# Other PSUM banks for the key norms, the query norms and the value transposes of two attention layers

## The reference

```python
x = x + attn_a(layernorm(x))   # q,k,v = z @ w(1024->64) @ fc(64->1024) + b ; 16 heads of 64
x = x + ffn(layernorm(x))      # 1024 -> 4096, gelu, -> 1024
x = x + attn_b(layernorm(x))   # q,k,v = x @ w_qkv ; 16 heads of 64
x = x + ffn(layernorm(x))

scores = einsum('bihd,bjhd->bhij', q, k) / 8
attn   = softmax(scores, axis=-1)
out    = einsum('bhij,bjhd->bihd', attn, v) @ fco_w + fco_b
```

## Time and profile before

| | us |
|---|---|
| profiled execution, its own time | 3357.94 |
| its span, first to last instruction, slowest core (6) | 3356.5 |
| spans of the eight cores | 3337.6 to 3356.5 |
| timed runs | 3369.16 and 3596.16, median 3482.66 |

### The profile page before, as it was taken

The page is one execution under the profiler, slowest core; times in us unless marked ns, Lnnn a source line. Parts: engine busy times, 40 slices in busy tenths (PEclk is TensorE's granted clock), DMA queues, the critical chain, the costliest instruction groups (busy, mean ns, idle before and its releaser), DMA issues.

```text
span 3356.5 us, 33712 instructions; the slowest of 8 cores (3337.6 to 3356.5 us)
## 1 busy us (share of the span) xinstructions
PE 2611.3 (78%) x10548; PEld 911.5 (27%) x10664; DVE 1121.0 (33%) x1570; ACT 1601.9 (48%) x1800; POOL 64.3 (2%) x122
## 2 busy tenths in 40 slices
PE   5557878687865698898947878787787863989999
PEld 1111222122221243343313322222222221334344
DVE  4543445344433021210253334444444432112010
ACT  2248989798920313212213239894898800320310
POOL 0000000000000000000000000000000000000000
PEclk8657999799987899999968889999899996999999
DMA  3000000000004625224001110001000017533532
GB/s 114 0 1 8 5 3 5 2 5 4 4 14 76 120 37 101 51 51 76 1 13 26 20 26 4 4 4 28 4 4 4 5 20 134 102 70 72 104 72 51
DMA packets 36263, 121.01 MB, mean 36 GB/s; under 512 B 7936, under 2 KB 12032, under 8 KB 26880
## 3 DMA queue, kind: packets, MB, share of 16 engines
q0 software_dynamic: 20832, 97.53, 16.9%
q1 hardware_dynamic: 12384, 12.93, 1.3%
q10 hardware_dynamic: 2880, 8.39, 0.7%
HBM read 203.50 MB, written 8.39 MB: 63 GB/s over the span
## 4 chain that ended last, share of the span: by engine, by line
PE 57%; ACT 16%; DVE 11%; DMA 7%; issue 6%; another core or an unknown queue 3%; DVEq 0%; ACTq 0%; SPq 0%; POOLq 0%; POOL 0%
ACT POOL L469 13%; PE PS_A L694 5%; PE PS_A L408 5%; PE PS_A L721 5%; PE PS_B L721 5%; PE PS_B L694 5%; DMA POOL<-w_h 5%; PE PS_C L484 3%; PE PS_D L721 3%; PE PS_D L484 3%; DVE sstat L139 2%; PE PS_C L488 2%; DVE SCR L139 2%; PE PS_E L488 2%
## 5 line engine op out<-in xcount | busy, mean ns | idle before, releaser
L469 ACT ACTIVATE POOL<-PS_A,ebias 128x1024 bf16<-128x1024 f32 x512 | 570.4, 1114 | 104.3 <-PE PS_C L488 40.8
L469 ACT ACTIVATE POOL<-PS_B,ebias 128x1024 bf16<-128x1024 f32 x512 | 570.2, 1114 | 21.6 <-PE PS_C L488 8.1
L694 PE MATMUL PS_A<-BIG,POOL 128*128 128x512 bf16 x1000 | 250.8, 393 | 155.3 <-DMA POOL<-w_h 128.1
L143 ACT ACTIVATE BIG<-PS_A,bcols 128x512 bf16<-128x512 f32 x144 | 98.9, 687 | 557.2 <-PE PS_A L694 543.5
L408 PE MATMUL PS_A<-BIG,POOL 64*128 64x512 bf16 x512 | 196.3, 383 | 102.3 <-ACT POOL L469 100.7
L694 PE MATMUL PS_B<-BIG,POOL 128*128 128x512 bf16 x1004 | 243.9, 383 | 1.2 <-issue 0.2
L408 PE MATMUL PS_B<-BIG,POOL 64*128 64x512 bf16 x512 | 196.1, 383 | 58.8 <-ACT POOL L469 56.9
L139 DVE SCALAR_TENSOR_TENSOR X<-PS_A,bcols,X 128x512 f32<-128x512 f32 x56 | 42.0, 750 | 587.2 <-PE PS_A L721 461.1
L484 PE MATMUL PS_C<-POOL 128*65 128x512 bf16 x512 | 213.2, 416 | 30.4 <-DVE SCR L139 30.4
L139 DVE RECIPROCAL PF<-SCR 33x512 f32<-33x512 f32 x64 | 214.1, 3345 | 67.3 <-DMA SCR<-PF 67.3
L484 PE MATMUL PS_D<-POOL 128*65 128x512 bf16 x512 | 206.9, 404 | 6.1 <-ACT POOL L469 6.1
(11 more groups left out here) (154 smaller groups left out, 3009.6 us busy)
## 6 DMA issues: line engine op xcount, KB each, us to landing
POOL<-w_h POOLq DMA_DIRECT2D x64, 1024.0 KB, 8.8
POOL<-w_h POOLq DMA_DIRECT2D x2, 8192.0 KB, 54.7
X<-xT SPq DMA_DIRECT2D x4, 1024.0 KB, 22.0
X<-xT ACTq DMA_DIRECT2D x4, 1024.0 KB, 25.2
BIG<-POOL SPq DMA_DIRECT2D x64, 64.0 KB, 1.9
POOL<-wqkv_kv POOLq DMA_DIRECT2D x16, 256.0 KB, 4.2
POOL<-wqkv_q POOLq DMA_DIRECT2D x16, 256.0 KB, 3.5
yT<-X SPq DMA_DIRECT2D x16, 256.0 KB, 2.4
```

Of the source, the lines that this page charges most:

```text
L143: return p.inc(getattr(nc.scalar, name)(*a, **k), "act", 1)
L469: nc.scalar.activation(psb, PSx[:, :], AF.Exp, bias=ebias[:, c:c + 1], scale=0.125),
L694: tt = nc.tensor.matmul(PSx[:, ucoff:ucoff + 512], wg[:, dc * 512 + j * 128: dc * 512 + j * 128 + 128], BIG2[:, hoff(dc):hoff(dc) + 512], ...
```

## The change

In `emit_knorm` all four slices go into one bank, PS_E, and each matmul waits for the maximum of the slice before it. The wait for everything issued to TensorE stays only in the first chunk; later chunks wait for named matmuls of the chunk before. `emit_vtranspose` goes through three banks, PS_C low, PS_C high and PS_D, and waits in each round for whoever last read that bank, over the passes too; its wait at the start for everything on VectorE stays only in the first chunk. The query norms alternate between the two banks of PS_A in place of PS_D and PS_E.

```diff
+        vt_bank_ev = {}
+        def emit_vtranspose(vts_off, cpair, entry=False):
-            p.wait(nc.tensor, "dve")
             p.wait(nc.tensor, "act")
+            if entry:
+                p.wait(nc.tensor, "dve")
+            banks = [PS_C[:, 0:512], PS_C[:, 512:1024], PS_D[:, 0:512]]
             for r4 in range(4):
-                boff = (r4 % 2) * 512
-                if r4 >= 2:
-                    p.wait(nc.tensor, round_eng[r4 - 2], round_ev[r4 - 2])
+                bi = r4 % 3
+                g = vt_bank_ev.get(bi)
+                if g is not None:
+                    p.wait(nc.tensor, g[0], g[1])
...
+                vt_bank_ev[bi] = ("dve" if r4 % 2 == 0 else "act", v)

+        kn_prev = {}
         def emit_knorm(cpair, sq_off):
-            p.wait(nc.scalar, "te")
+            if cpair == 0:
+                p.wait(nc.scalar, "te")
+                kn_prev.clear()
             p.wait(nc.scalar, "dve")
-            psl = [PS_D[0:1, 0:512], PS_E[0:1, 0:512]]
...
-                if sl >= 2:
-                    p.wait(nc.scalar, "te", tmm[sl - 2])
+                g = tmm.get(sl - 2) or kn_prev.get("t%d" % (sl + 2))
+                if g is not None:
+                    p.wait(nc.scalar, "te", g)
                 sq = sop("activation", ksq, kc_ap, AF.Square)
                 p.wait(nc.tensor, "act", sq)
-                if sl >= 2:
-                    p.wait(nc.tensor, "dve", mx[sl - 2])
-                tmm[sl] = p.inc(nc.tensor.matmul(psl[sl % 2], ones_b[:, 0:1],
-                                                 ksq, start=True, stop=True),
+                gm = mx.get(sl - 1) or kn_prev.get("m3")
+                if gm is not None:
+                    p.wait(nc.tensor, "dve", gm)
+                tmm[sl] = p.inc(nc.tensor.matmul(PS_E[0:1, 0:512],
+                                                 ones_b[:, 0:1], ksq,
+                                                 start=True, stop=True),
                                 "te", 1)
...
         def emit_qnorm2_and_ebias(sq_off):
-            psl = [PS_D[0:1, 0:512], PS_E[0:1, 0:512]]
+            psl = [PS_A[0:1, 0:512], PS_A[0:1, 512:1024]]
```

More of the change, by code:

```diff
@@ L295, in emit_layernorm_exp @@
             return out
-        def emit_vtranspose(vts_off, cpair):
-            p.wait(nc.tensor, "dve")
+        vt_bank_ev = {}
+        def emit_vtranspose(vts_off, cpair, entry=False):
             p.wait(nc.tensor, "act")
-            round_ev = {}
-            round_eng = {}
+            if entry:
+                p.wait(nc.tensor, "dve")
+            banks = [PS_C[:, 0:512], PS_C[:, 512:1024], PS_D[:, 0:512]]
             for r4 in range(4):
-                boff = (r4 % 2) * 512
-                if r4 >= 2:
-                    p.wait(nc.tensor, round_eng[r4 - 2], round_ev[r4 - 2])
+                bi = r4 % 3
+                g = vt_bank_ev.get(bi)
+                if g is not None:
+                    p.wait(nc.tensor, g[0], g[1])
                 for j in range(4):
                     kt = r4 * 4 + j
-                    psv = PS_C[:, boff + j * 64: boff + (j + 1) * 64].bitcast(BF16)
+                    psv = banks[bi][:, j * 64:(j + 1) * 64].bitcast(BF16)
                     src = POOL[:, vts_off + kt * 128: vts_off + kt * 128 + 128]
@@ L325, in emit_vtranspose @@
                         v = sop("activation", da, sa, AF.Identity)
-                round_ev[r4] = v
-                round_eng[r4] = "dve" if r4 % 2 == 0 else "act"
+                vt_bank_ev[bi] = ("dve" if r4 % 2 == 0 else "act", v)
             return p.cnt["dve"]
+        kn_prev = {}
         def emit_knorm(cpair, sq_off):
-            p.wait(nc.scalar, "te")
+            if cpair == 0:
+                p.wait(nc.scalar, "te")
+                kn_prev.clear()
             p.wait(nc.scalar, "dve")
-            psl = [PS_D[0:1, 0:512], PS_E[0:1, 0:512]]
             tmm = {}
@@ L336, in emit_knorm @@
             for sl in range(4):
-                ksq = POOL[:, (sq_off if sl % 2 == 0 else MB + 8192):
-                           (sq_off if sl % 2 == 0 else MB + 8192) + 512]
+                off = sq_off if sl % 2 == 0 else MB + 8192
+                ksq = POOL[:, off:off + 512]
                 kc_ap = KAR[:, cpair * T + sl * 512: cpair * T + sl * 512 + 512]
-                if sl >= 2:
-                    p.wait(nc.scalar, "te", tmm[sl - 2])
+                g = tmm.get(sl - 2) or kn_prev.get("t%d" % (sl + 2))
+                if g is not None:
+                    p.wait(nc.scalar, "te", g)
                 sq = sop("activation", ksq, kc_ap, AF.Square)
                 p.wait(nc.tensor, "act", sq)
-                if sl >= 2:
-                    p.wait(nc.tensor, "dve", mx[sl - 2])
-                tmm[sl] = p.inc(nc.tensor.matmul(psl[sl % 2], ones_b[:, 0:1],
-                                                 ksq, start=True, stop=True),
+                gm = mx.get(sl - 1) or kn_prev.get("m3")
[4 more added lines that the diff above has]
+                                                 start=True, stop=True),
                                 "te", 1)
                 p.wait(nc.vector, "te", tmm[sl])
-                mx[sl] = vop("reduce_max", S_KSL(sl), psl[sl % 2], axis=AX.X)
+                mx[sl] = vop("reduce_max", S_KSL(sl), PS_E[0:1, 0:512],
+                             axis=AX.X)
             vop("reduce_max", S_KMAX(cpair), sstat[0:1, 16:20], axis=AX.X)
+            kn_prev["t2"] = tmm[2]
+            kn_prev["t3"] = tmm[3]
+            kn_prev["m3"] = mx[3]
         def emit_qnorm2_and_ebias(sq_off):
@@ L812, in build @@
                 p.wait(nc.tensor, "act")
-                emit_vtranspose(OA_VTS, c)
+                emit_vtranspose(OA_VTS, c, entry=(c == 0))
             kv_done = p.cnt["dve"]
@@ L921, in build @@
                 emit_knorm(c, OB_SQ)
-                emit_vtranspose(OB_VTS, c)
+                emit_vtranspose(OB_VTS, c, entry=(c == 0))
             kvb_done = p.cnt["dve"]
```

## The result

| | before | changed kernel |
|---|---|---|
| timed runs, median | 3372.47 us (39 runs) | 3393.64 us (40 runs) |
| profiled execution, its own time | 3357.94 us | 3384.37 us |
| key/value stage, layer A, slowest core | 125.1 us | 139.1 us |
| key/value stage, layer B, slowest core | 195.7 us | 206.4 us |

The ratio of changed to before is 1.0065, with a 95% interval of 1.0049 to 1.0080: slower by 0.65%. The interval leaves out 1, so the change is slower, but by far less than 2%.

The account below looks back on a forecast made before the run. The two key/value stages were taken as chains of handovers with no engine full. 3357.94 + 19.9 - 6.4 + 6.6 = 3378.0 us, +0.6%; range 3354 to 3404 us, 95% within 2% of no change.

Parts of the forecast that it names:

- rival 1: Key norms, both layers: the one-bank turn is hidden and only the gains stay, time 3339.5 us; chance 4%.
- rival 2: Layer B: TensorE's clock stays down, 12.5 us a pass, 100 in eight, time 3478 us; chance 3%.
- rival 3: Whole program: the change is absorbed because something later was waiting anyway, time 3358 us; chance 3%.
- I hold to the profiled execution: Base of the sum: the profiled execution's 3357.94 us, not 3482.66, the median of two unlike timed runs.
- I take 0, in the middle: Layer B, TensorE's clock: cost put at 0 us, between +12 from above and -11 from below.
- Key norms, layer A: One-bank norms: three turns of 1.62 us, last norm matmul 2.49 us later, nothing covers it; eight passes, +19.9 us.
- Third bank, layer A: Transposes: round 2's copies and the next keys come 0.80 us earlier a pass; eight passes, -6.4 us.
- The narrower waits ... are 0 as well: Key norm's start: narrower waits on ScalarE gain nothing, since the remaining VectorE wait covers key copies; 0 us.
- Both edits, layer B: Norms' 2.17 us two thirds paid back by removed wait and third bank; next keys 0.82 later a pass, +6.6 us.
- Query norms: Query norms keep two alternating banks, only others, and the PS_A halves are free then; 0 us.
- The upper bound: Layer B clock: seven more passes with the longer low stretch, 3.4 us dense work at half speed, 1.7 each, +12.
- the predicted signs: Trace marks of being right (turns 1.6 us, stages 138.6 and 202.3) or wrong (stage B above 215, loop over pairs beyond 10).

Follow-up runs that it names:

- the filled kernels: Changed kernel, and the same with two-bank key norms, each with throwaway matmuls in TensorE's idle time in layer B: ratios to before 0.9999 and 0.9919.
- a fourth kernel: Kernel before with one edit: the transposes' start wait for all of VectorE stays only in the first pass; ratio 0.9968, stage B 191.2 us.

## Why the prediction was right or wrong

**The reason and the difference held, the time did not.** Forecast was +20.1 us on the profiled execution, a ratio of 1.0060; measured is 1.0065 (1.0049 to 1.0080). The rivals are out: the turn is not hidden, stage A alone is 14.0 us longer (rival 1; the 0.995 that its 3339.5 stands for was measured, but only with the turn taken away); the clock came back in every pass, if later (rival 2); nothing was absorbed, the two stages grew by 24.6 us and the rest of the program by 1.9 (rival 3).

**Two steps failed. The first is the base of the sum, "I hold to the profiled execution".** The time came out 15.6 us above the forecast, 3393.64 against 3378.0. The base, 3357.94, was 14.5 us under the median that 39 runs of before then gave, 3372.47, and that is nearly the whole gap. Set beside the median of the first two runs, 3482.66, 3378.0 even reads as a gain of 3%, which the working never said; that median is no base for a change of this size. A forecast of a small change should be read as a difference, and its base named as the weakest number in it. **The second is the clock term, "I take 0, in the middle"**, where layer B lost some 4 us more (below).

Term by term, measured against the forecast:

- *Key norms, layer A*, +19.9: three turns of 1.59, not 1.62, so 2.39 a pass or +19.1. The one-bank kernel alone measured +19.2.
- *Third bank, layer A*, -6.4: 0.77 to 0.80 a pass in the timeline, as forecast, but the passes kept only 0.6 of it. With the third bank and the start wait in every pass the stage was 5.1 us shorter, for the guards of the banks are waits too: from the start of the last value eviction to the first transpose it is 1.15 us there, where it was 1.05.
- *"The narrower waits ... are 0 as well"*: wrong by 0.16 a pass, +1.1 us. They are narrower but there are more of them, and each met wait takes its place in the queue (137.9 against 139.1 us). The dropped start wait gives 0.7 us in layer A when it is the only edit; in the changed kernel the banks' guards stand in its place, and the way to the first transpose is 1.08 us, no shorter than the 1.05 of before. Stage A was forecast at 138.6 and measured at 139.1 because these small errors nearly cancel.
- *Both edits, layer B*, +6.6: the way from first norm to next keys grew by 0.5 us (7.15 to 7.66), not by 0.8, since a turn at the upper clock takes 1.37 and the clock in that pass held through three of the four norms; the met wait adds 0.1 ahead of it, and the short passes as a whole are the 0.8 longer that the walk gave (24.9 against 24.1). The long ones are a further 1.5 us.
- *The clock, "I take 0, in the middle"*: this term was mis-sized. Stage B grew by 10.65 us (195.72 to 206.37; the medians of the eight cores, 196.0 and 206.7, say the same), where the walk without the clock had 6.6: 4 us more. About 3 of them are the 5.9 us more of keys at the lower level in passes 2 to 8; the rest was not added up, but turns at the lower level are longer (1.59 us, not 1.37) and three of the seven gaps now have most of their norms there, where one had. The upper bound rests on a misreading as well. It charged every longer low stretch 3.4 us of dense work, 1.7 us of time. The longer stretches did come, six of the seven between passes on this core last 10.2 us where six of seven had lasted 6.8, but half of them begin earlier and lie over the thin part, where no dense work is slowed. Only in passes 3, 5 and 7 did the keys wait longer for the clock, and that is where the passes of 25.7 to 26.5 us come from. The rows that the bound was read from say the same: in the 10.2 us of 1766.8 to 1777.0 the keys run for the last 3.8 us alone.
- *Query norms*, 0: right, ratio 1.0063 with them undone.

On the Trainium skill's rule that cycling through PSUM banks can keep TensorE's clock falling and rising ("TensorE: Matmul & The Clock Gate", section "A second HAM failure mode: psum-queue depth-cycling"): the trace agrees more than I allowed. The rule would have put the sum nearer 3390 on the same base, a rise of 32 us; the stages together rose by 24.6, between that and the 20.1 of the rows. The same page's section "HAM oscillation — how this bites in real kernels" advises, for matmuls with few rows that wait for transfers, to restructure the loop so that TensorE stays warm. No loop was restructured here; what a clock that stays up is worth the filled kernels show, 17.6 us in 206, from matmuls whose results nobody reads.

What the predicted signs said: norm matmuls 1.6 us apart (1.59), a pass of A of 17.2 (17.3), stage A at 138.6 (139.1), round 2's copies 0.1 behind round 0's (0.10) all came in; stage B at 202.3 did not (206.4), though it stayed below the 215 named as a sign of being wrong. No stretch outside the two stages moved by the 10 us named either.

## What to carry to other kernels

When a small result is summed by one engine and read by another, the second PSUM bank is what lets the two overlap: with one bank each slice costs matmul plus reader plus two handovers, here 1.59 us in place of 0.78, and every engine's busy time stays the same. So freeing a bank for one stage has to be priced at its old user; here the bank did not even have to be taken away, since both users fit with one guard. And where dense TensorE stretches alternate with thin ones, a change in the gap acts twice, on its own and through the clock, so list the passes one by one before trusting their mean.

## What the runs showed of the hardware that was not expected

- Adding 176 matmuls to a stage made it 17.6 us shorter (206.4 to 188.8), as the granted clock went from 0.81 to 0.99.
- The later passes in layer B settled at 23.8 to 24.1 us on all eight cores in two kernels with different gaps, because the keys of the one with the shorter gap ran 1.1 us longer at the lower level. In the changed kernel passes alternated between 24.9 and 26.3 to 26.5 us, again on all eight cores; in a fourth kernel the cores differed (23.9 on most, 21.6 and 23.3 on one).
- A semaphore wait that is already met costs 0.06 us on ScalarE and 0.11 us on TensorE if it stands in a chain of handovers: 0.16 us a pass for the pair, 1.2 us in stage A.
